# Loads of the residual rows in a three-stage kernel: issued by GpSimd instead of SyncE

## The chip, the cores and the metric

The kernel runs on one core of a Trainium2 chip. The metric is the device time of one execution in microseconds; for the kernel before it is the median of three runs. A core has TensorE (PE, matmuls), VectorE (DVE), ScalarE (ACT), GpSimd (POOL) and SyncE (SP), each with an instruction stream of its own that runs in order. They wait for each other by semaphores. SyncE does no arithmetic here; it issues DMAs. ACT issues DMAs as well, between its activations. All transfers of the core run on the same 16 DMA engines.

## The reference

The inputs are x and a context of 32 sequences x 512 rows x 512 columns, and a feed-forward layer with 2048 hidden columns.

```
r_t  = 0.9 * r_(t-1) + ctx_t * ctx_t              # scan over the 512 rows of a sequence
x2   = x + layernorm(x) * r
a    = quantize_uint8(layernorm(x2))              # one scale: the maximum over everything
h    = relu(a @ quantize_int8(w1).T + bq1)
hq   = quantize_uint8(h)                          # one scale: the maximum over everything
out  = x2 + hq @ quantize_int8(w2).T + bq2
```

The two scales cut the work into three stages: x2 must be complete before its quantized form can be made, and h must be complete before its own.

## The kernel before

Stage one (to about 349 us) makes x2 of every sequence and stores it in `x2_scratch` in HBM; GpSimd does small row statistics here and nothing afterwards. Stage two (to about 830 us) loads x2 again, quantizes it, forms the first product and keeps its unscaled sums in pieces that the text calls pairs: 128 partitions x 1024 fp32, 512 KB, 8 of them for a sequence. Those of 30 sequences go to `hidden_scratch` in HBM (240 pairs), those of the last two, the held ones, stay in SBUF.

Stage three, in which the change lies, walks over the sequences in turns, the two held ones first. In a turn s:

- ACT scales and rounds 8 pairs, half a pair per activation (L589), into a ring `hq` of 12 halves. Pairs come from a ring `hload` of 30 places. After the second half of a pair ACT issues the load of the pair 13 places on in the order of HBM (L570), and this one is needed 29 pairs later, since 16 held pairs lie ahead of all of them. The first 14 are loaded by SyncE before the stage, the other 226 by ACT in this way.
- PE forms the second product: 64 matmuls of 128x512 (L877), into four of the eight PSUM banks; turns take the two halves of PSUM by turns, so turn s may write a bank when DVE has read it for turn s - 2.
- DVE adds the bias to the x2 of the turn (`add_bias`, L761), then takes the sums from PSUM (`scale_out`, L752) and adds them (`add_out`, L766), four row tiles each. In DVE's stream stand, for turn s, first all outputs of turn s - 1, then `add_bias` of turn s.
- x2 of a turn lies in one of three slots of `work`. The result is formed in the same slot and stored from there. So the slot of turn s + 3 is free for its load only when the store of turn s has landed.

Loads (L349) and stores (L353), 1.05 MB each, are both issued by SyncE, in one stream: the store of turn s, then, after a wait for that store to land, the load of turn s + 3, then the store of turn s + 1. The last turn is stored in four parts (L370). The load of turn 2 (x2 of turns 0 and 1 is there from stage two) is issued ahead of the loop.

Of the kernel before, what the change touches and what calls it, by code (L numbers as in the profile page):

```python
# [39 lines left out]
HELD = 2  # L40
# [8 lines left out]
def wait_count(eng, sem, count):  # L49

    if isinstance(count, int) and count <= 0:
        return
    eng.wait_ge(sem, count)


def build(nc, x, ctx_in, w1, b1, w2, b2, out):
    NB, S, D = x.shape
    F = w1.shape[0]
    NI = S // P
# [8 lines left out]
    turns_c = held + stored  # L68
# [5 lines left out]
    def copy_index(b, q):  # L74
        return copied.index(b) * NP2 + q
# [11 lines left out]
    x2_dram = nc.dram_tensor("x2_scratch", [NB, P, ROW], F32, kind="Internal").ap()  # L87

    with ExitStack() as es:
# [3 lines left out]
        def sem(name):  # L93
            return es.enter_context(nc.semaphore(name))
# [63 lines left out]
        x2c = x2t  # L158
# [58 lines left out]
        x_scaled = sem("x_scaled")  # L217
# [13 lines left out]
        x2c_loaded = [sem(f"x2c_loaded{n}") for n in range(3)]  # L231
        bias_added = sem("bias_added")
        out_ready = sem("out_ready")
        out_stored = [sem(f"out_stored{n}") for n in range(3)]
# [6 lines left out]
        def batches(eng, step, peeled=0):  # L241

            for j in range(STRAIGHT):
                step(j, j % XS, j // XS)
            with eng.Fori(AHEAD, NG - peeled) as g:
                for n in range(XS):
                    step(g * XS + n, n, g)
            for j in range(NB - peeled * XS, NB):
                step(j, j % XS, j // XS)

        def is_first(j, n=1):
            return isinstance(j, int) and j < n

        def load_ctx(eng, j, n):
            eng.dma_start(ct[n], ctx_rows[bass.ds(j, 1)].rearrange("b p i d -> (b p) i d")).then_inc(ctx_loaded[n], 16)

        def weight_halves(j):

            at = {1: (0, 0), 2: (0, 1), 5: (1, 0), 6: (1, 1)}.get(j) if isinstance(j, int) else None
            return [at] if at else []  # L260
# [15 lines left out]
        def stores_in(n):  # L276

            return len(range(n, NLOAD, NKEEP))

        def out_slot(s):  # L280

            return (NB - HELD + s) % 3
# [5 lines left out]
        def stores_until(s):  # L288

            return len([m for m in range(s + 1) if out_slot(m) == out_slot(s)])  # L290
# [10 lines left out]
        @block.sync  # L301
        def _(sp):
            def store_x2(j, n):
                sp.wait_ge(x2_done, (j + 1) * NI)
                sp.dma_start(x2_dram[bass.ds(j, 1)].rearrange("b p m -> (b p) m"),
                             xt[n].rearrange("p i d -> p (i d)")).then_inc(x2_stored[n], 16)

            def load_x2(t):
                sp.dma_start(x2t[t % 3].rearrange("p i d -> p (i d)"), x2_dram[t]).then_inc(x2_loaded[t % 3], 16)

            def phase_a(j, n, g):
                if is_first(j):
                    load_ctx(sp, 0, 0)
                if isinstance(j, int) and j == XS - 1:
                    sp.wait_ge(dve_step, 1)
                if not is_first(j, XS):
                    sp.wait_ge(x2_stored[n], g * 16)
                sp.dma_start(xt[n], x_rows[bass.ds(j, 1)].rearrange("b p i d -> (b p) i d")).then_inc(x_loaded[n], 16)
                for w, h in weight_halves(j):
                    rows = (NF, KD)[w]  # L320
                    part = slice(h * rows // 2, (h + 1) * rows // 2)
                    sp.dma_start(w_stage[w].rearrange("p (c d) -> p c d", c=rows)[:, part, :],
                                 (w1_rows, w2_rows)[w][:, part, :]).then_inc(w_loaded[w][h], 16)
                if isinstance(j, int) and j == 2:
                    sp.dma_start(brow[:, :], b1_rows).then_inc(b_loaded, 16)
                    sp.dma_start(brow2[:, :], b2_rows).then_inc(b_loaded, 16)
                if not is_first(j, 2):
                    store_x2(j - 2, (n - 2) % XS)

            batches(sp, phase_a)  # L330
            store_x2(NB - 2, XS - 2)
            store_x2(NB - 1, XS - 1)
            sp.wait_ge(w_int, 8)
            for t in range(3):
                load_x2(t)

            for n, b in enumerate(stored):
                for q in range(NP2):
                    c = copy_index(b, q)
                    sp.wait_ge(h_copied, c + 1)  # L340
                    sp.dma_start(h_dram[n, q], hkeep[c % NKEEP].rearrange("p n t -> p (n t)")).then_inc(h_stored[c % NKEEP], 16)


            def load_x2c(s):
                if stores_until(s) > 1:
                    sp.wait_ge(out_stored[out_slot(s)], 16 * (stores_until(s) - 1))
                else:
                    sp.wait_ge(x_scaled, (NB - 2) * NI)
                sp.dma_start(x2c[out_slot(s)].rearrange("p i d -> p (i d)"), x2_dram[turns_c[s]]).then_inc(x2c_loaded[out_slot(s)], 16)  # L349

            def store_out(s):
                sp.wait_ge(out_ready, (s + 1) * NI)
                sp.dma_start(out_rows[turns_c[s]], x2c[out_slot(s)]).then_inc(out_stored[out_slot(s)], 16)  # L353

            for n in range(NKEEP):
                sp.wait_ge(h_stored[n], 16 * stores_in(n))
            sp.wait_ge(kept_maxed, NLOAD)
            for c in range(NKEEP):
                sp.dma_start(hload[c].rearrange("p n t -> p (n t)"), h_dram[c // NP2, c % NP2]).then_inc(h_loaded[c], 16)
            for s in range(HELD, 3):  # L360
                load_x2c(s)
            for s in range(len(turns_c) - 1):
                store_out(s)
                if s + 3 < len(turns_c):
                    load_x2c(s + 3)

            last = len(turns_c) - 1
            for i in range(NI):
                sp.wait_ge(out_ready, last * NI + i + 1)
                sp.dma_start(out_rows[turns_c[last], :, i, :], x2c[out_slot(last)][:, i, :]).then_inc(tail_stored, 16)  # L370
            sp.wait_ge(tail_stored, 16 * NI)
            for n in range(3):
                sp.wait_ge(out_stored[n], 16 * len([m for m in range(last) if out_slot(m) == n]))
# [3 lines left out]
        def _(gp):  # L377
# [18 lines left out]
            def row_stats(pw, st, mean, done, base):  # L396

                n = st.shape[1]
                me, mo, ve, vo = (st[:, :, k] for k in (1, 4, 2, 5))
                t = [pw[:, k, :] for k in range(8)]  # L400
                gp.tensor_tensor(t[0], me, mo, ALU.add)
                gp.tensor_tensor(t[1], ve, vo, ALU.add)
                gp.tensor_tensor(t[2], me, mo, ALU.subtract).then_inc(done, 1)
                gp.wait_ge(done, base + 1)
                gp.tensor_tensor(mean, t[0], half[:, 0:n], ALU.mult)
                gp.tensor_tensor(t[3], t[1], per_row[:, 0:n], ALU.mult)
                gp.tensor_tensor(t[4], t[2], half[:, 0:n], ALU.mult).then_inc(done, 1)  # L407
                gp.wait_ge(done, base + 2)
                gp.tensor_tensor(t[5], t[3], eps[:, 0:n], ALU.add)  # L409
                gp.tensor_tensor(t[6], t[4], t[4], ALU.mult).then_inc(done, 1)  # L410
                gp.wait_ge(done, base + 3)
                gp.tensor_tensor(t[7], t[5], t[6], ALU.add).then_inc(done, 1)  # L412
                return t[7]

            def second_stats(j, n):

                cols = bass.ds(j * NI, NI)
                wait_count(gp, stats2_ready, j)
                gp.wait_ge(stats2_in, j + 1)
                mean = pw2[:, 8, :]  # L420
                var = row_stats(pw2, st2[:, n], mean, ln2_step, j * 4)
                gp.wait_ge(ln2_step, j * 4 + 4)
                gp.tensor_tensor(pw2[:, 9, :], var, var, ALU.add)
                gp.tensor_tensor(zrow[:, cols], rowmax[:, n, :], mean, ALU.subtract).then_inc(stats2_used, 1)  # L424
                gp.tensor_tensor(mean2[:, cols], pw2[:, 0, :], half[:, :], ALU.mult)
                gp.tensor_tensor(rstd2[:, cols], var, neg_half[:, :], ALU.pow).then_inc(stats2_ready, 1)  # L426
# [23 lines left out]
            batches(gp, phase_a)  # L450
            second_stats(NB - 2, XS - 2)
            second_stats(NB - 1, XS - 1)


        @block.scalar
# [466 lines left out]
```

## Time and profile before

| | us |
|---|---|
| median of 3 runs (lowest, highest) | 1315.63 (1314.29, 1317.24) |
| the profiled execution | 1313.3 |
| its span, first to last instruction | 1311.5 |

| engine | busy us | share of the span | instructions |
|---|---|---|---|
| PE | 1229.3 | 94% | 5386 |
| ACT | 993.6 | 76% | 1403 |
| DVE | 908.9 | 69% | 1314 |
| POOL | 291.2 | 22% | 777 |

The DMA engines moved 460.23 MB, 351 GB/s over the span. Busy time counts instructions on an engine's datapath; waits and DMA issues are not in it, and have rows of their own ("SPq", "ACTq") in the timeline. Matmuls are pipelined, so a row of the timeline that merges many gives their time in sum better than a mean of single ones. A view by windows gives for each stretch the busy time of each engine with the number of instructions in it, then the granted clock, the DMA share and GB/s. In a wait, "A <- B" means that A stood idle until B released it; B is inferred, and a time in which an engine's own queue was held by a DMA issue can be put down to another engine.

### The profile page before, as it was taken

The page shows a single profiled execution, that of the slowest core. Times are in us where ns is not written, and L with a number is a line of the kernel's source. Part 1 is how long each engine was busy: PE and PEld are TensorE (multiplying, and loading weights), DVE is VectorE, ACT ScalarE, POOL GpSimd, SP SyncE. Part 2 cuts the span into 40 slices and gives each one's busy share as a digit, 9 for nine tenths or more (in the row PEclk, how much of TensorE's full clock was granted, in tenths as well). Part 3 has the DMA queues.
Part 4 walks back from the last instruction along what each step waited for, and adds up shares of the span by engine and source line. Part 5 has one row for each costly group of instructions (what it writes and reads, how often), then busy time and mean ns, then how long its engine had stood idle before and what let it go on. Part 6 is the DMA issues. An engine that isn't in the chain of part 4 may idle for free.

```text
span 1311.5 us, 17101 instructions
## 1 busy us (share of the span) xinstructions
PE 1229.3 (94%) x5386; PEld 562.2 (43%) x5386; DVE 908.9 (69%) x1314; ACT 993.6 (76%) x1403; POOL 291.2 (22%) x777
## 2 busy tenths in 40 slices
PE   6768999999599999999999999799999999989998
PEld 3333434343344444444444444344444444333333
DVE  5979999999577777777777777465454444444466
ACT  6687878787677777777777776778888787787774
POOL 2969999999500000000000000000000000000000
PEclk9888999999799999999999999899999999999999
DMA  9987999997489999999999998699999999999986
GB/s 355 343 325 261 344 332 346 339 334 287 193 308 362 352 350 362 364 357 345 362 362 362 350 355 322 227 354 417 415 415 416 415 415 416 416 415 415 416 297 219
DMA packets 136128, 460.23 MB, mean 351 GB/s; under 512 B 10853, under 2 KB 10873, under 8 KB 123513
## 3 DMA queue, kind: packets, MB, share of 16 engines
q1 hardware_dynamic: 82968, 277.91, 54.1%
q10 hardware_dynamic: 53088, 181.42, 39.1%
q8 instruction: 39, 0.64, 0.2%
q14 instruction: 33, 0.26, 0.0%
HBM read 266.35 MB, written 192.94 MB: 350 GB/s over the span
## 4 chain that ended last, share of the span: by engine, by line
PE 50%; DMA 18%; POOL 18%; issue 6%; DVE 4%; ACT 3%; POOLq 1%; ACTq 0%; DVEq 0%; SPq 0%
PE ps L835 34%; PE ps L877 12%; DMA out_dram<-work 12%; DMA work<-x_scratch 6%; PE ps L857 2%; POOL rstd L426 2%; POOL pw L410 2%; POOL pw L412 2%; POOL pw L409 2%; DVE work L766 2%; PE ps L814 1%; POOL rstd L444 1%; DVE work L761 1%; POOL pw L407 1%; POOL zrow L424 1%
## 5 line engine op out<-in xcount | busy, mean ns | idle before, releaser
L877 PE MATMUL ps<-w2T,xq 128*128 128x512 f16 x2048 | 451.9, 381 | 17.6 <-DVE work L752 9.9
L835 PE MATMUL ps<-xq,w1T 128*128 128x512 f16 x2048 | 449.4, 380 | 1.4 <-DVE xq L713 1.4
L589 ACT ACTIVATE xq<-xq,hb,hs 128x512 f16<-128x512 f32 x494 | 359.3, 802 | 92.9 <-PE ps L877 81.3
L704 DVE TENSOR_REDUCE work<-xq 128x2 f32<-128x1024 f32 x255 | 311.0, 1220 | 126.6 <-ACT xq L542 126.6
L542 ACT ACTIVATE xq<-ps 128x1024 f32<-128x1024 f32 x255 | 261.2, 1024 | 123.0 <-PE ps L835 122.8
L814 PE MATMUL ps<-xq,work 128*128 128x512 f32 x640 | 290.0, 610 | 30.1 <-ACT xq L477 19.7
L877 PEld LDWEIGHTS ps<-w2T,xq 128*128 128x128 f16 x2048 | 197.9, 98 | 271.6 <-ACT xq L589 21.9
L835 PEld LDWEIGHTS ps<-xq,w1T 128*128 128x128 f16 x2048 | 199.5, 98 | 237.4 <-issue 2.9
L814 PEld LDWEIGHTS ps<-xq,work 128*128 128x128 f32 x640 | 122.4, 195 | 195.3 <-issue 144.5
L761 DVE TENSOR_TENSOR work<-work,bq_bc 128x512 f32<-128x512 f32 x128 | 79.8, 685 | 165.4 <-DMA work<-x_scratch 165.4
L477 ACT ACTIVATE xq<-ps,rstd 128x512 f32<-128x512 f32 x128 | 78.0, 689 | 60.4 <-POOL rstd L444 56.0
L752 DVE TENSOR_TENSOR work<-ps,cs_bc 128x512 f32<-128x512 f32 x128 | 86.1, 687 | 48.9 <-PE ps L877 41.7
L622 DVE SCALAR_TENSOR_TENSOR xq<-xq,mean 128x512 f32<-128x512 f32 x128 | 96.1, 791 | 21.6 <-ACT xq L477 21.5
L548 ACT ACTIVATE work<-work,qb,zrow 128x512 f16<-128x512 f32 x128 | 102.6, 806 | 5.1 <-DVE qb L695 2.8
L630 DVE CUSTOM_DVE_ANT_0 xq<-xq 128x512 f32<-128x512 f32 x128 | 88.2, 689 | 0.0
L766 DVE TENSOR_TENSOR work<-work 128x512 f32<-128x512 f32 x128 | 84.7, 681 | 0.4
L627 DVE BATCH_NORM_STATS2 st<-xq 128x6 f32<-128x512 f32 x128 | 84.6, 681 | 0.0
L507 ACT ACTIVATE xq<-xq 128x2048 f32<-128x2048 f32 x32 | 60.8, 1899 | 6.1 <-DMA xq<-in_ctx_dram 5.8
L655 DVE BATCH_NORM_STATS2 st<-xq 128x6 f32<-128x512 f32 x64 | 40.4, 672 | 9.6 <-DMA xq<-in_x_dram 9.6
L468 ACT ACTIVATE work<-xq,st 128x512 f32<-128x512 f32 x64 | 45.3, 707 | 0.0
L465 ACT ACTIVATE work<-xq 128x512 f32<-128x512 f32 x64 | 40.8, 637 | 4.6 <-DMA xq<-in_x_dram 3.6
L713 DVE COPY xq<-ps 128x2048 f16<-128x2048 f16 x32 | 38.9, 1214 | 2.5 <-PE ps L857 2.5
(103 smaller groups left out, 536.7 us busy)
## 6 DMA issues: line engine op xcount, KB each, us to landing
hidden_scratch<-xq SPq DMA_DIRECT2D x240, 512.0 KB, 6.0
xq<-hidden_scratch ACTq DMA_DIRECT2D x218, 512.0 KB, 19.5
work<-x_scratch SPq DMA_DIRECT2D x33, 1024.0 KB, 8.3
xq<-in_x_dram SPq DMA_DIRECT2D x32, 1024.0 KB, 7.7
x_scratch<-xq SPq DMA_DIRECT2D x32, 1024.0 KB, 5.8
xq<-in_ctx_dram ACTq DMA_DIRECT2D x31, 1024.0 KB, 5.5
out_dram<-work SPq DMA_DIRECT2D x31, 1024.0 KB, 15.1
work<-x_scratch ACTq DMA_DIRECT2D x29, 1024.0 KB, 7.7
```

Source lines behind the costliest of these rows:

```text
L542: act.activation(into, pair_banks(b, q), ACT.Copy).then_inc(h_copied, 1)
L548: act.activation(qi[:, i, :], x2t[t % 3][:, i, :], ACT.Relu, bias=qb[:, t * NI + i:t * NI + i + 1], scale=qa[:, t * NI + i:t * NI + i + 1] ...
L589: act.activation(hq[c % HQ], src[:, c % 2, :], ACT.Relu, bias=hb[:, q:q + 1], scale=hs[:, q:q + 1]).then_inc(h_scaled, 1)
L622: dve.scalar_tensor_tensor(rs[n % 2][:, i, :], xt[n][:, i, :], mean1[:, n, i:i + 1], rs[n % 2][:, i, :], ALU.subtract, ALU.mult).then_inc( ...
L630: dve.tensor_tensor_reduce(xt[n][:, i, :], rs[n % 2][:, i, :], xt[n][:, i, :], 1.0, -3.0e38, ALU.add, ALU.max, rowmax[:, n, i:i + 1]).then ...
L704: dve.tensor_reduce(hmax[:, b * NF + 2 * q:b * NF + 2 * q + 2], src, AX.X, ALU.max).then_inc(kept_maxed, 1)
L752: dve.tensor_tensor(ot[:, i % 2, :], acc_bank(s, i), cs2_bc[:, :], ALU.mult).then_inc(acc_read, 1)
L761: dve.tensor_tensor(x2c[out_slot(s)][:, i, :], x2c[out_slot(s)][:, i, :], bq2_bc[:, :], ALU.add).then_inc(bias_added, 1)
L766: dve.tensor_tensor(x2c[out_slot(s)][:, i, :], x2c[out_slot(s)][:, i, :], ot[:, i % 2, :], ALU.add).then_inc(out_ready, 1)
L814: last = pe.matmul(ps[:, i, :], decay_mat[:, (i - k) * P:(i - k + 1) * P], ct[n][:, k, :], start=(k == 0), stop=(k == i))
L835: last = pe.matmul(bank, w1T[:, k, f * P:(f + 1) * P], xq_rows(b, k), start=(k == 0), stop=(k == KD - 1))
L877: last = pe.matmul(acc_bank(s, i), src[:, i * P:(i + 1) * P], w2T[:, q, :], start=first, stop=final)
```

## The change

The function `load_x2c` and the loop that calls it for turns 2 to 31 move from SyncE's stream to the end of GpSimd's. The waits in it are the same: for turn 2 that ACT has scaled 30 sequences in stage two, for the others that the earlier store out of that slot has landed. SyncE keeps the stores, and the waits of DVE are as they were.

```diff
-            def load_x2c(s):
-                if stores_until(s) > 1:
-                    sp.wait_ge(out_stored[out_slot(s)], 16 * (stores_until(s) - 1))
-                else:
-                    sp.wait_ge(x_scaled, (NB - 2) * NI)
-                sp.dma_start(x2c[out_slot(s)].rearrange("p i d -> p (i d)"), x2_dram[turns_c[s]]).then_inc(x2c_loaded[out_slot(s)], 16)
-
...
-            for s in range(HELD, 3):
-                load_x2c(s)
             for s in range(len(turns_c) - 1):
                 store_out(s)
-                if s + 3 < len(turns_c):
-                    load_x2c(s + 3)
...
             second_stats(NB - 2, XS - 2)
             second_stats(NB - 1, XS - 1)
+
+            def load_x2c(s):
+                if stores_until(s) > 1:
+                    gp.wait_ge(out_stored[out_slot(s)], 16 * (stores_until(s) - 1))
+                else:
+                    gp.wait_ge(x_scaled, (NB - 2) * NI)
+                gp.dma_start(x2c[out_slot(s)].rearrange("p i d -> p (i d)"), x2_dram[turns_c[s]]).then_inc(x2c_loaded[out_slot(s)], 16)
+
+            for s in range(HELD, len(turns_c)):
+                load_x2c(s)
```

## Rows read from the trace of the kernel before

**Rows 1.** Windows, stage three; last columns: clock, DMA share, GB/s
```profile
868.00:1262.00 394.00, 379.76 (x1734) 166.91 (x1733) 193.83 (x311) 314.41 (x432) 0.00 (x0) 1.00 1.03 414
920.00:960.00 40.00, 40.00 (x187) 18.15 (x186) 20.38 (x32) 33.06 (x47) 0.00 (x0) 1.00 1.03 415
1262.00:1311.50 49.50, 42.84 (x197) 18.73 (x194) 35.98 (x58) 28.86 (x40) 0.00 (x0) 0.99 0.67 215
```

**Rows 2.** PE: chain of waits (first row), timeline: start, us, work
```profile
852.64 112.25 PE ps L877 x520
...
1102.50 0.39 PE L877 MATMUL ps<-w2T,xq 128*128 128x512 f16 x1 [0.53 <-ACT xq L589]
1106.49 2.94 PE L877 MATMUL ps<-w2T,xq 128*128 128x512 f16 x12 [0.30 <-DVE work L752]
1263.57 2.94 PE L877 MATMUL ps<-w2T,xq 128*128 128x512 f16 x12 [0.68 <-DVE work L752]
1266.87 39.02 PE L877 MATMUL ps<-w2T,xq 128*128 128x512 f16 x180 [0.35 <-DVE work L752]
```

**Rows 3.** Waits in stage three: us in total, times, longest
```profile
DVE work L761 <- DMA work<-x_scratch: 165.4, 25, 8.9
ACT xq L589 <- PE ps L877: 83.6, 64, 3.2
```

**Rows 4.** Timeline of SyncE's queue, two turns
```profile
983.85 0.43 SPq L353 DMA_DIRECT2D out_dram<-work  x1
999.79 0.33 SPq L349 DMA_DIRECT2D work<-x_scratch  x1
1000.16 0.43 SPq L353 DMA_DIRECT2D out_dram<-work  x1
```

**Rows 5.** DMA issues of 870 to 1242; last: landing of L349 after 1262
```profile
work<-x_scratch SPq DMA_DIRECT2D x24, 1024.0 KB, 8.3
out_dram<-work SPq DMA_DIRECT2D x24, 1024.0 KB, 15.4
...
DMA to landing us min/median/max: 6.1/6.3/6.5
```

**Rows 6.** Timeline of ACT and its queue
```profile
1082.44 4.07 ACTq L570 DMA_DIRECT2D xq<-hidden_scratch  x1
1086.61 0.81 ACT L589 ACTIVATE xq<-xq,hb,hs 128x512 f16<-128x512 f32 x1 [2.80 <-PE ps L877]
1086.66 1.58 ACTq L570 DMA_DIRECT2D xq<-hidden_scratch  x1
...
1093.04 0.33 ACTq L570 DMA_DIRECT2D xq<-hidden_scratch  x1
```

**Rows 7.** Queues (q10 ACT, q1 SyncE): packets, MB, share; to 1242, to 1312
```profile
q10 hardware_dynamic: 31308, 114.03, 70.5%
q1 hardware_dynamic: 16067, 49.97, 30.9%
...
q10 hardware_dynamic: 32544, 118.50, 62.5%
```

**Rows 8.** Windows of L589 (ACT, first two) and L877 (PE) alone
```profile
838.00:1100.00 262.00, 215.46 (x300) 0.99 1.01 402
838.00:1242.00 404.00, 326.81 (x451) 0.99 1.02 407
...
838.00:1100.00 262.00, 260.18 (x1193) 116.96 (x1193) 0.99 1.01 402
838.00:1242.00 404.00, 389.67 (x1769) 171.06 (x1769) 0.99 1.02 407
```

**Rows 9.** Timeline of DVE: the end of turn 0's output, and the last
```profile
860.40 1.28 DVE L766 TENSOR_TENSOR work<-work 128x512 f32<-128x512 f32 x2
...
1308.33 0.69 DVE L766 TENSOR_TENSOR work<-work 128x512 f32<-128x512 f32 x1
```

**Rows 10.** The page's 40 slices of the span: GpSimd
```profile
POOL 2969999999500000000000000000000000000000
```

## The prediction, made before the changed kernel was run

> **Words.** A turn is one sequence's second product: 64 matmuls and 16 ACT activations. It takes 8 pairs (512 KB each) of kept sums, which ACT loads, one x2 load and one output store of 1.05 MB each. Turns 0 and 1 need no loads of pairs; 226 pairs come through ACT's queue.
>
> **What bounds the kernel now.** I read the stage table first. From 868 to 1262 us the DMA engines are full: 415 GB/s in a 40 us slice, DMA share 1.03; PE is busy 96% of it. After 1262 they carry 215 GB/s [rows 1]. So the third stage has two bounds close together. PE runs free at 112.25 us for 520 matmuls, 0.2159 us each: 13.81 us a turn. It does so until 1102.50, where ACT first releases it; turn 19 starts at 1106.49 and turn 29 at 1263.57, 15.7 us each [rows 2]. The DMA bound is 8 x 0.524 + 2 x 1.049 = 6.29 MB a turn, 15.15 us at 415.
>
> Next, the waits: DVE stood 165.4 us for x2 loads [rows 3]. The SyncE timeline shows why. After the store at 983.85 SyncE does nothing until 999.79, issues the load, and 0.37 us later the next store, without a wait of its own [rows 4]: it was ready. The load of turn s+3 waits for the landing of store s (its slot), and store s+1 is queued behind that wait. A store lands in 15.4 us, a load in 8.3 [rows 5], both in one queue: one turn in about 15.7 us, whatever PE does.
>
> Third, and this decides the case: ACT's own queue. At 1082.44 issuing one pair load takes 4.07 us, at 1086.66 1.58; one that isn't held takes 0.33 (1093.04). The activation behind the first starts only at 1086.61 [rows 6], when the issue is over; the 2.80 us the view puts down to PE is this. So ACT is held when its queue is full. How full: by 1242 all 226 pairs are issued and 114.03 of 118.50 MB have landed [rows 7], so 4.47 MB are outstanding, 8.5 pairs. Yet pair loads are issued 29 pairs ahead of use: the data needed is there, and ACT stands in an issue. ACT's lead over PE: at 1100 it has started 302 activations (300 in the window, 2 ahead of it), 151.0 pairs, and PE 1194 matmuls (1193 and 1), 149.25 pairs: a lead of 1.75, and there PE's first stalls stand. At 1242 it is 226.5 against 221.25, a lead of 5.25 [rows 8]. ACT, then, was the limit around 1100, and from there DVE's x2 waits were.
>
> **The change, part by part.** (1) Removed from SyncE: 30 loads and their waits. Issue time is 0.33 us each, hidden in idle time, worth nothing. What counts is that store s+1 no longer waits for store s to land. It goes out when ready: 4.9 us after its turn's last matmul (turn 0's end is 856.8, that is 843 + 13.81 where 843 is 964.89 less 565 x 0.2159; DVE was done at 861.68 [rows 9]).
>
> (2) Added to GpSimd: 30 waits and 30 issues. GpSimd does nothing after its eleventh slice [rows 10]; nothing is queued behind its waits but further loads, whose slots are freed later. The first load, for turn 2, now goes out when the 30th sequence is scaled, before stage two ends; its data is used after 870. Worth nothing. Without an idle GpSimd each wait of some 10 us would stand ahead of its arithmetic.
>
> (3) What a load costs in GpSimd's queue no row shows. The nearest rows from both sides: 6.3 us landed in a quiet stretch, 15.4 for a store behind a load in a full one [rows 5]. A store alone in its queue should land in 6.5 to 9. Store s plus load s+3 take 9 + 8.3 + 1, or 9 + 15.4 + 1 = 25.4 us; the load is needed when turn s+2 is done, two turns or 27.6 us after store s was ready. So DVE's x2 waits go, with 2 to 9 us to spare. I take 8.3, its own row.
>
> (4) What is late next. With DVE out of the way SyncE and GpSimd move 2.10 MB in each turn of PE instead of one turn's worth in 15.7 us. At PE's free pace that leaves 415 x 13.81 - 2097 = 3634 KB for pairs, 6.9 where 8 are asked for. ACT's queue fills by 1.1 pairs a turn and its issues hold ACT. Before, x2 and output had 49.97 MB by 1242 [rows 7], about 1.8 MB in 13.81 us, and it filled by 0.5 a turn. So ACT falls behind sooner, at about turn 10 to 12 instead of 19, and then the pace is the DMA bound, 15.15 us.
>
> **The sum.** Let X be the time of the last pair issue, after which nothing holds ACT; before, 1241.8. By X the same pairs must have moved as before. Of x2 and output more has moved: with PE then at pair 224.75, turn 28.1 (ACT at 226.5, less the lead of 1.75 that a held ACT has), stores 0 to 26 and loads 3 to 28 have landed, 53 x 1.0486 = 55.6 MB, against 49.97. These 5.6 MB at 0.415 MB/us are 13.5 us: X = 1255.3. Left for PE are 256 - 224.75 = 31.25 pairs of 1.726 us, 53.9 us: PE ends at 1309.2. Before: 34.75 pairs, 60.0 us, from 1241.8 gives 1301.8, and 4.1 us of waits for DVE to the real end, about 1305.9 (39.02 us from 1266.87 [rows 2]). The drain behind PE (DVE's last work starts at 1308.33 [rows 9]) stays. So +3.3 us: the span goes from 1311.5 to 1314.8, the profiled execution from 1313.3 to 1316.6. The median shown is 2.3 above that execution; I forecast 1318.9 for it, +0.25%. What was gained at DVE is handed back because x2 traffic that was late, and finished in the half empty tail, now competes with the pairs.
>
> Errors of the sum: a lead off by half a pair, 0.9 us; one pair more outstanding at X (a load fewer in SyncE's and ACT's queues may leave room), 1.3 us less; a data rate off by 1%, 385 us of full traffic, 3.9 us. This case: 1313 to 1323.
>
> **Rivals.** A, faster: ACT isn't held any more, because the limit on its issues is shared with SyncE and the loads leave it. Then the lag of 1.1 pairs over 26 turns is 28 pairs, within the 29 issued ahead, and PE could run free to 843 + 32 x 13.81 = 1284.9. The bytes allow hardly less: left at 1242 are 4.5 MB of pairs [rows 7] and, of 32 stores and 29 loads (64.0 MB), 14.0 MB; less the last 1.6 that is 16.9 MB, 41 us, so 1283, and some 10 us for the last pair and the drain. A span of 1293, a median near 1297. Against it speaks that an issue of 1.58 us [rows 6] is about what a pair takes in the engines (0.524 MB at 415 less SyncE's share), so each issue waits for one pair to leave its own queue. For it, that SyncE's transfers may take the same places; no row tells. 12%.
>
> B, no change: a load in GpSimd's queue lands so late (over 27 us) that DVE waits on, and the pace stays 15.7. The row of 15.4 speaks against it. 1315.6, 8%. The Trainium skill has a rule with the same result: all engines' DMAs run on the same 16 DMA engines, and issuing from several saves only issue time (DMA: Bandwidth & Descriptors, Issuing engines are not separate DMA queues). By that rule the change is worth 0.33 us a turn beside idle time, nothing. The trace agrees about the shared engines (415 GB/s is full), but shows an order of waits in SyncE's stream that the rule doesn't speak of.
>
> C, slower by more: the third queue lowers the rate of all. Its place is the full stretch; 1% costs 3.9 us, and it decides from the first per cent on. The slice shown holds 415 [rows 1]; 2% gives 1327, 4% 1334. 18%. The Trainium skill says that DMA engines 7 and 15 are usually slower and guesses at descriptor rings that GpSimd writes into SBUF (DMA: Bandwidth & Descriptors, Latency and other measured facts); a pair load is done when its slowest engine is. No row here has such a queue.
>
> **How the numbers follow.** My case has 62%. 0.2%, 2.6 us, is about what a measurement of this kernel can tell from no change. In my case +3.3 with an error of about 3 gives 0.34 slower, 0.22 same, 0.06 faster. With A 0.12 faster, B 0.08 same, C 0.18 slower: 0.18, 0.30, 0.52. The range, 1309 to 1332, leaves out A and the far end of C.
>
> **What would show it.** Right: stores follow DVE's last work by under 1 us; GpSimd's loads start as a store lands; DVE's waits for x2 loads fall from 165 us to under 20; ACT's issues are longer in sum, the first over 1 us before 960; PE's stalls begin near 1000, released by ACT and not DVE; last pair issue near 1255; 415 GB/s held until about 1270, then a shorter tail. Wrong: issues of 0.33 us throughout (A), 160 us of DVE waits (B), 40 us slices at 405 GB/s or less (C).

## The result, and the profile after

| | before | after |
|---|---|---|
| median, us | 1315.56 (9 runs, 1312.85 to 1317.24) | 1318.06 (9 runs, 1317.53 to 1319.27) |
| ratio, 95% interval | | 1.0029 [1.0018, 1.0039] |
| span of the profiled execution, us | 1311.5 | 1315.7 |

The change makes the kernel slower by 0.29%. That is small, but the whole interval lies above 1. The transfers move as the change says. From the page of the changed kernel (span; GpSimd in 40 slices; the new queue with packets, MB and share):

```profile
span 1315.7 us, 17101 instructions
POOL 2859999999500000000000000000000000000000
...
q0 software_dynamic: 4320, 31.46, 5.8%
```

The 30 loads have left SyncE's queue for GpSimd's (q0, 31.46 MB), and GpSimd's busy share rounds to nothing after its eleventh slice, as in [rows 10] (the windows below count its issues as POOL: 27 in the full stretch, 14.52 us). The windows of stage three, in answer to [rows 1]:

```profile
868.00:1262.00 394.00, 376.37 (x1711) 165.71 (x1709) 204.36 (x324) 304.88 (x423) 14.52 (x27) 1.00 1.03 416
...
1262.00:1315.70 53.70, 48.14 (x224) 21.61 (x221) 27.96 (x44) 36.03 (x51) 1.08 (x2) 0.98 0.51 191
```

The full stretch carries 416 GB/s with a third queue in it, as much as with two. After 1262 the engines are emptier than before, 191 GB/s instead of 215: less was left over for the tail. PE is busy 376.37 us of the 394, against 379.76.

The waits of stage three, in answer to [rows 3] (us in total, times, longest):

```profile
POOL work L448 <- DMA out_dram<-work: 486.4, 29, 97.6
DVE work L751 <- PE ps L876: 209.3, 63, 8.2
ACT xq L588 <- PE ps L876: 84.4, 43, 4.2
PE ps L876 <- ACT xq L588: 19.4, 31, 2.0
```

DVE's 165.4 us of waits for x2 are gone from the list; what DVE waits for now is PE. PE waits for ACT, 31 times. The full list has no row in which ACT waits for a DMA from `hidden_scratch`: the pairs it needs are there.

DVE's last work of a turn, SyncE's store of it, GpSimd's next two loads with what released them, and then the landing times of the stores (L346) and of the loads (L448):

```profile
969.05 1.28 DVE L765 TENSOR_TENSOR work<-work 128x512 f32<-128x512 f32 x2
...
970.36 0.37 SPq L346 DMA_DIRECT2D out_dram<-work  x1
...
972.12 0.54 POOL L448 DMA_DIRECT2D work<-x_scratch  x1 [13.96 <-DMA out_dram<-work]
984.49 0.54 POOL L448 DMA_DIRECT2D work<-x_scratch  x1 [11.83 <-DMA out_dram<-work]
...
DMA to landing us min/median/max: 4.3/13.9/15.4
...
DMA to landing us min/median/max: 5.0/9.3/10.7
```

DVE ends at 970.33 and the store is issued at 970.36. The load at 984.49 follows 0.3 us after this store has landed, 14.1 us after its issue; the load at 972.12 was released by the store of the turn before. This answers [rows 4, 5]: no store waits for another one.

ACT and its queue, in answer to [rows 6]; the last row is the last pair issue of the kernel:

```profile
948.40 1.62 ACTq L569 DMA_DIRECT2D xq<-hidden_scratch  x1
...
1244.75 5.48 ACTq L569 DMA_DIRECT2D xq<-hidden_scratch  x1
...
1250.33 0.81 ACT L588 ACTIVATE xq<-xq,hb,hs 128x512 f16<-128x512 f32 x1 [4.20 <-PE ps L876]
...
1255.32 0.33 ACTq L569 DMA_DIRECT2D work<-hidden_scratch  x1
```

The first issue of over 1 us comes at 948.40; before the change it was at 1004.63. The one at 1244.75 takes 5.48 us and the activation behind it starts when it is over, at 1250.33. In sum the 226 issues take 149.5 us beyond 0.33 us each; before, 115.8. From 985 us to 1245 one issue in each turn takes 4.2 to 5.9 us and a few behind it 1 to 2 us; the stops of PE below come once a turn too.

PE in stage three, in answer to [rows 2]:

```profile
853.22 152.65 PE L876 MATMUL ps<-w2T,xq 128*128 128x512 f16 x706
1007.07 0.39 PE L876 MATMUL ps<-w2T,xq 128*128 128x512 f16 x1 [1.19 <-ACT xq L588]
1007.77 13.77 PE L876 MATMUL ps<-w2T,xq 128*128 128x512 f16 x63 [0.32 <-ACT xq L588]
...
1129.48 0.39 PE L876 MATMUL ps<-w2T,xq 128*128 128x512 f16 x1 [1.08 <-ACT xq L588]
...
1144.81 0.39 PE L876 MATMUL ps<-w2T,xq 128*128 128x512 f16 x1 [0.86 <-ACT xq L588]
...
1251.20 0.39 PE L876 MATMUL ps<-w2T,xq 128*128 128x512 f16 x1 [1.44 <-ACT xq L588]
1251.91 58.23 PE L876 MATMUL ps<-w2T,xq 128*128 128x512 f16 x269 [0.31 <-ACT xq L588]
```

PE runs free to three quarters of turn 11 (152.65 us) and is then released by ACT, in most turns once, with a further small stop of 0.3 us. From 1129.48 to 1144.81 is one turn, 15.3 us; the 16 turns from 1007.07 to 1251.20 take 15.26 each. Before, PE ran free 95 us longer and then lost 1.9 us a turn. In that stage the waits of the kernel before put 9.9 us of PE's idle time down to DVE (19 times) and 5.1 to ACT (7 times); that this pace was set by DVE's wait for x2 is shown by serial_free below.

The queues at 1255 us (q10 ACT, q1 SyncE, q0 GpSimd), then the windows of ACT's activations and of PE's matmuls up to there, in answer to [rows 7, 8]:

```profile
q10 hardware_dynamic: 31227, 113.74, 68.0%
q1 hardware_dynamic: 14236, 28.30, 17.5%
q0 software_dynamic: 3744, 27.26, 15.7%
...
838.00:1255.00 417.00, 326.15 (x452) 0.99 1.01 407
...
838.00:1255.00 417.00, 396.52 (x1794) 174.26 (x1795) 0.99 1.01 407
```

### The profile page after: what moved, and what is told of

It reads as the page before. It is cut to its first block and busy times, and to the rows that moved or that the text cites. A ratio compares the mean times of both kernels' runs of the same rounds, so it can differ in the third digit from the quotient of the medians.

```text
span 1315.7 us, 17101 instructions
## 1 busy us (share of the span) xinstructions
PE 1230.5 (94%) x5386; PEld 563.6 (43%) x5386; DVE 910.7 (69%) x1314; ACT 990.8 (75%) x1403; POOL 307.2 (23%) x807
## 3 DMA queue, kind: packets, MB, share of 16 engines
q0 software_dynamic: 4320, 31.46, 5.8%
## 5 line engine op out<-in xcount | busy, mean ns | idle before, releaser
L448 POOL DMA_DIRECT2D work<-x_scratch x30 | 16.4, 545 | 912.5 <-DMA out_dram<-work 486.4
## 6 DMA issues: line engine op xcount, KB each, us to landing
xq<-hidden_scratch ACTq DMA_DIRECT2D x218, 512.0 KB, 20.1
out_dram<-work SPq DMA_DIRECT2D x31, 1024.0 KB, 13.9
```

## The experiments

Two theories. **H**, for "held": PE is limited by ACT, and ACT is held in the issues of its own full queue, for pairs that it needs only 29 pairs later. The change frees DVE, but makes x2 traffic prompt, which fills ACT's queue sooner; so one hold takes the place of the other. **D**, for "data": PE goes at the pace at which bytes arrive, and the held issues are a symptom. Both give the changed kernel's 15.2 us a turn. They part where ACT no longer issues the pairs.

With the first three kernels the two holds can be set out in a table, each taken away alone and both together (medians, us; each ratio is to the kernel before as it ran beside that kernel, where its median was 1315.56 for the changed kernel and 1314.96 for the other three; so a difference between medians of the two groups is uncertain by some 0.6 us):

| | ACT issues the pairs | another engine issues them |
|---|---|---|
| SyncE's serial order | before: 1315.6 | serial_free: 1312.1, 0.9982 [0.9972, 0.9992] |
| stores and x2 loads prompt | after: 1318.1, 1.0029 [1.0018, 1.0039] | act_freed: 1295.6, 0.9856 [0.9832, 0.9880]; pairs_gp: 1297.5, 0.9877 [0.9852, 0.9902] |

### act_freed: ACT issues the stores, SyncE the pairs

```diff
 SyncE, instead of the stores:
+            for c in range(NKEEP, NLOAD):
+                sp.wait_ge(h_scaled, 2 * (c - NKEEP + 1))
+                sp.dma_start(hload[c % NRING]..., h_dram[c // NP2, c % NP2]).then_inc(h_loaded[c % NRING], 16)
 ACT, in its loop over half pairs c:
-                if c % 2 == 1 and NKEEP <= pair + NKEEP - 1 < NLOAD:
-                    load_kept(pair + NKEEP - 1)
+                if c % NF == 3 and c >= 2 * NF:
+                    store_out(c // NF - 2)
```

> The changed kernel, with the two hardware queues swapped between their issuers: SyncE issues the 226 pair loads, ACT issues the 31 output stores (that of turn s after the fourth activation of turn s + 2, when it is ready) and the four last parts; GpSimd keeps the x2 loads. The bytes are the same. Theory H (the changed kernel's ACT is held in its pair issues by its full queue, while the pairs it needs lie ready; x2 traffic is prompt): ACT is free, SyncE is held instead and holds nobody, PE runs at 13.8 us a turn to near the end, and the bytes are the bound: 1293 to 1301 us. Theory D (PE simply goes at the pace at which bytes arrive, 15.2 us a turn, and the held issues are a symptom without effect): no change from the changed kernel, 1316 to 1320.

Measured: 1295.64 us, 22.4 less than the changed kernel. Its PE, then its waits in stage three, then the window of the full stretch:

```profile
853.80 415.00 PE L875 MATMUL ps<-w2T,xq 128*128 128x512 f16 x1922
1269.64 0.39 PE L875 MATMUL ps<-w2T,xq 128*128 128x512 f16 x1 [0.84 <-ACT xq L582]
...
ACT xq L582 <- DMA xq<-hidden_scratch: 13.2, 18, 2.5
PE ps L875 <- ACT xq L582: 4.3, 5, 2.0
...
868.00:1282.00 414.00, 412.84 (x1912) 186.92 (x1911) 228.09 (x360) 338.63 (x470) 15.67 (x29) 1.00 1.03 416
```

PE runs 415 us without a stop, until near the end of stage three. The DMA engines carry the same 416 GB/s as in the changed kernel. So, as long as the reserve lasts, PE isn't tied to the pace at which bytes arrive: it takes 13.8 us a turn where a turn's bytes take 15.2, and lives on the 29 pairs of reserve that ACT's hold kept it from using in the changed kernel. D falls. SyncE is held now (147 of its 226 issues take over 1 us), and holds nobody. Only near the end, from 1207 us on, does ACT wait for pairs that haven't landed, 13.2 us in all; there the bytes begin to bind. This version beats both kernels.

### serial_free: the kernel before, GpSimd issues the pairs

```diff
 GpSimd, at its end:
+            for c in range(NKEEP, NLOAD):
+                gp.wait_ge(h_scaled, 2 * (c - NKEEP + 1))
+                gp.dma_start(hload[c % NRING]..., h_dram[c // NP2, c % NP2]).then_inc(g_loaded[c % NRING], 16)
 ACT:
-                if c % 2 == 1 and NKEEP <= pair + NKEEP - 1 < NLOAD:
-                    load_kept(pair + NKEEP - 1)
```

> The kernel before, with the 226 pair loads issued by GpSimd instead of ACT; SyncE keeps stores and x2 loads in its old order. Theory H: ACT is free, but the order in SyncE (each store waits for the one before to land) still paces DVE at about 15.7 us a turn, so taking away ACT's hold alone is worth little: 1308 to 1317, with some 150 us of DVE waits for x2 and PE released by DVE. Theory D: 1314 to 1318, the same as before. A rival S, that SyncE's order never limited and ACT's hold alone did: 1293 to 1301.

Measured: 1312.05 us. PE, and the waits:

```profile
854.64 268.66 PE L879 MATMUL ps<-w2T,xq 128*128 128x512 f16 x1244
1123.55 11.40 PE L879 MATMUL ps<-w2T,xq 128*128 128x512 f16 x52 [0.25 <-DVE work L754]
1136.81 2.94 PE L879 MATMUL ps<-w2T,xq 128*128 128x512 f16 x12 [1.86 <-DVE work L754]
...
1262.34 2.94 PE L879 MATMUL ps<-w2T,xq 128*128 128x512 f16 x12 [1.21 <-DVE work L754]
...
DVE work L763 <- DMA work<-x_scratch: 155.7, 24, 8.9
PE ps L879 <- DVE work L754: 11.0, 17, 1.9
```

The first stop moves from 1102.50 to 1123.55, and it is DVE that ends it; DVE's waits for x2 are 155.7 us, against 165.4. From 1136.81 to 1262.34 are eight turns of 15.7 us, the pace of the kernel before, though no pair issue stands in ACT's stream. So ACT's hold was worth 2.4 us in the kernel before (1.1 to 3.7 by the interval of the ratio), and SyncE's order takes over 21 us later. This is H. S falls; D's no change is missed by only 2 us, and it is act_freed that decides against D.

### pairs_gp: GpSimd issues the pairs, ACT the x2 loads, SyncE the stores

```diff
 ACT:
+                if c % NF == 4 and c >= 3 * NF:
+                    load_x2c(c // NF)
```

with the loads of the pairs on GpSimd as above.

> Three issuers another way round: GpSimd the 226 pair loads, SyncE the stores alone, ACT the x2 loads (that of turn s after the fifth activation of turn s, when the slot's store should have landed). Neither SyncE's order nor a full ACT queue is left. Theory H: as with ACT freed in the other way, 1293 to 1301. Theory D: 1314 to 1320. If a queue filled by GpSimd costs rate, this kernel, with 118 MB in it instead of 30, is slower than the other by several us, and a full stretch shows under 410 GB/s.

Measured: 1297.47 us. PE, and the window of the full stretch:

```profile
852.65 387.37 PE L883 MATMUL ps<-w2T,xq 128*128 128x512 f16 x1794
1240.34 0.39 PE L883 MATMUL ps<-w2T,xq 128*128 128x512 f16 x1 [0.32 <-ACT xq L595]
...
868.00:1282.00 414.00, 411.63 (x1901) 185.37 (x1900) 225.19 (x356) 338.15 (x468) 111.23 (x207) 1.00 1.03 415
```

Nearly the same gain in another arrangement (1.8 us less of it), so it isn't a property of SyncE's or ACT's queue. With four times as many bytes in GpSimd's queue as in the changed kernel the engines carry 415 GB/s. None of GpSimd's issues takes over 1 us, though its pairs land in 32.8 us in the median (20.1 in the changed kernel).

### quarter: the changed kernel with a quarter of each x2 load

```diff
-                gp.dma_start(x2c[out_slot(s)].rearrange("p i d -> p (i d)"), x2_dram[turns_c[s]])...
+                gp.dma_start(x2c[out_slot(s)][:, 0, :], x2_dram[turns_c[s]][:, 0:D])...
```

> The changed kernel with only one of four row tiles of each x2 load in stage three (262 KB instead of 1.05 MB; the other three tiles of the slot keep what lay there, so the output lacks part of x2). A turn moves 5.5 MB, 13.3 us at 415 GB/s, under PE's 13.8. Both theories H and D: ACT isn't held for long, PE runs free, its end is near 839.7 + 1.8 + 442 = 1284, the median 1291 to 1295. It measures what the x2 traffic costs in the changed kernel: some 24 us. A rival N, that something in GpSimd's queue other than its bytes holds PE: over 1305.

Measured: 1294.26 us. PE, the window, and the durations of ACT's issues (ns, min, median, max):

```profile
855.60 431.83 PE L876 MATMUL ps<-w2T,xq 128*128 128x512 f16 x2000
...
868.00:1262.00 394.00, 394.00 (x1827) 178.58 (x1826) 216.38 (x343) 327.38 (x456) 15.90 (x29) 1.00 0.97 378
...
L569 ACTq DMA_DIRECT2D xq<-hidden_scratch x218: 326/326/828, 840.6 to 1225.6; - x109
```

The output lacks three quarters of x2 here. With 23 MB less in the queues, PE's row runs over 2000 matmuls, no issue of ACT takes over 0.83 us, and the DMA share is 0.97. These bytes of x2 cost the changed kernel 23.8 us (1318.06 less 1294.26), though DVE waits for none of them. As act_freed carries all of them in 1295.6 us, they cost it through ACT's queue.

### early_wait: act_freed with a wait that ACT doesn't need

```diff
+                if c % 2 == 1 and NKEEP <= pair + 4 < NLOAD:
+                    act.wait_ge(h_loaded[(pair + 4) % NRING], 16 * ((pair + 4) // NRING + 1))
```

> The kernel in which SyncE issues the pair loads and ACT the stores (1295.6 us), plus one wait in ACT: after the second half of pair p it waits until the pair has landed that is used 20 pairs later, the one 9 issues behind the load that ACT itself would issue there. It makes ACT wait as a full queue of 8.5 pairs would, for data that it doesn't need yet; transfers and issuers stay. Theory H (it is this hold of ACT that costs the 22 us, not where the loads are issued): PE's stalls come back near turn 11 or 12, released by ACT, a turn takes 15.2 us, and the time is 1314 to 1321. Theory Q (the kernel was faster because pairs in SyncE's queue and stores in ACT's are served better): it stays under 1300.

Measured: 1316.18 us, ratio 1.0014 [1.0003, 1.0025]. PE, and the waits:

```profile
853.39 166.58 PE L877 MATMUL ps<-w2T,xq 128*128 128x512 f16 x771
1020.28 13.91 PE L877 MATMUL ps<-w2T,xq 128*128 128x512 f16 x63 [0.31 <-ACT xq L582]
...
1126.87 0.39 PE L877 MATMUL ps<-w2T,xq 128*128 128x512 f16 x1 [0.63 <-ACT xq L582]
...
1141.97 0.39 PE L877 MATMUL ps<-w2T,xq 128*128 128x512 f16 x1 [0.63 <-ACT xq L582]
...
DVE work L761 <- DMA work<-x_scratch: 116.0, 23, 7.0
ACT xq L582 <- DMA xq<-hidden_scratch: 59.1, 73, 2.2
PE ps L877 <- ACT xq L582: 16.6, 40, 2.0
```

The same transfers by the same issuers as in act_freed; one wait in ACT, for data used 20 pairs later, costs 20.5 us. PE's stops are back, released by ACT; 1126.87 to 1141.97 is 15.1 us. Q falls. The imitation isn't exact: ACT also issues the stores here, and where ACT is late they are late; DVE waits 116.0 us for x2, which it doesn't in the changed kernel. The list has no row in which PE waits for DVE, though.

### split_pairs: the changed kernel, each pair load as two halves

```diff
+                for h in range(2):
+                    act.dma_start(hload[c % NRING][:, h, :], h_dram[c // NP2, c % NP2][:, h * S:(h + 1) * S])...
```

> The changed kernel with each of ACT's pair loads issued as two of half a pair (256 KB, 2 KB a partition). It asks what fills the queue. If it is bytes: ACT is held again at 8.5 pairs, and the time is 1317 to 1320. If it is transfers or their pieces, twice as many for the same bytes: it is held at about 4.3 pairs, first before 925 us, the last issue comes some 5 us later for the bytes that are no longer outstanding, and the time is 1321 to 1327.

Measured: 1339.40 us, ratio 1.0186 [1.0164, 1.0208]: slower than both expectations. PE, the window of 1000 to 1200 us, and the landing of half pairs and stores:

```profile
855.03 69.71 PE L877 MATMUL ps<-w2T,xq 128*128 128x512 f16 x322
925.41 0.39 PE L877 MATMUL ps<-w2T,xq 128*128 128x512 f16 x1 [0.68 <-ACT xq L589]
...
1000.00:1200.00 200.00, 183.31 (x809) 76.76 (x808) 94.98 (x151) 150.68 (x204) 7.02 (x13) 1.00 1.05 401
...
xq<-hidden_scratch ACTq DMA_DIRECT2D x436, 256.0 KB, 11.2
out_dram<-work SPq DMA_DIRECT2D x31, 1024.0 KB, 9.6
```

Two things act. ACT is held with 8.2 half pairs outstanding in the median (4.3 to 10.2), 4.1 pairs; its first issue of over 1 us is at 853.15, and PE's first stop at 925.41. So it isn't bytes that fill the queue, but transfers, or pieces of them, of which half a pair has as many rows as a pair; the two aren't told apart. And the rate is 401 GB/s instead of 416, which I hadn't reckoned with: over 385 us of full traffic 3.7% is 14 us, and with the 5 us expected for the lower fill the sum is 1337. That these two terms make up the whole is worked out, not shown by a run.

## Why the prediction was right

The forecast was 1318.9 us, +3.3 by the sum; the medians differ by 2.5 and the spans by 4.2. Both the path (DVE freed, ACT held sooner, less left for the tail) and the size came out. Point by point:

- **The order of waits in SyncE** is gone, and with it DVE's 165 us. Forecast under 20 us, found none. The stores go out within 0.1 us of DVE's end.
- **What is late next: ACT's queue.** Forecast: first issue over 1 us before 960, PE's stalls from about turn 10 to 12, near 1000, released by ACT. Found: 948.40, turn 11, 1007.07, ACT. The pace of the DMA bound, 15.15 us a turn, was 15.26.
- **The balance of bytes at X.** Forecast: stores and x2 loads have moved 55.6 MB when the last pair is issued, X = 1255.3, and ACT's lead is 1.75 pairs. Found: 28.30 + 27.26 = 55.56 MB and 1255.32. The lead was 1.75 at 1255.00 (226 pairs, 452 halves, less 224.25, 1794 matmuls), but at the issue itself the counts are 453 and 1795, a lead of 2.1. So close an agreement in X is in part luck: the stage began 0.74 us later than in the trace of before (PE's long row starts at 853.22 instead of 852.48), and the rate was 416 instead of 415, which nearly cancels it.
- **PE's end.** Forecast 1309.2, found 1251.91 + 58.23 = 1310.1; 0.65 of the 0.9 us is that lead: at X PE was at pair 224.4 instead of 224.75. The late start is already in X. It is no more than scatter: in the eight kernels PE's long row starts between 852.48 and 855.60.
- **A term that was wrong: how fast a store lands.** I gave a store alone in its queue 6.5 to 9 us. It took 13.9 in the median, hardly less than the 15.4 it took behind a load. The load took 9.3, near the 8.3 chosen. Together with the issue of 0.54 that is 23.7 us of the 27.6 there were while PE ran free, so it cost nothing. With a load of 15.4, the upper bound of that part, it would have been 29.8: DVE would have waited until ACT was held, and from then on two turns give 30.5. The margin given as 2 to 9 us was about 4 with the measured landings, and below zero at that bound.
- **The rivals.** A (ACT isn't held any more) fell by the trace and is what act_freed then made, by other means: 1295.6, where A's sum said 1297. B fell: x2 loads land in 9.3 us. C fell: 416 GB/s, and 415 in pairs_gp with 118 MB in GpSimd's queue. The runs turned on an issuer's order of waits and on an issuer that is held: with the same transfers on the same engines, who issues them was worth 22 us. The Trainium skill's rule that issuing from several engines saves only issue time (DMA: Bandwidth & Descriptors, Issuing engines are not separate DMA queues) agrees with the rates here, 415 to 416 GB/s whoever issues. By it the change is worth nothing and act_freed as well; measured were +0.29% and -1.4%, so the time doesn't follow it, unless the time for which an issue is held, up to 5.86 us, is counted as issue time. Of the engines 7 and 15 that the Trainium skill calls usually slower (same page, Latency and other measured facts) no run shows a cost in the total rate.

What stays open: whether the queue is full by transfers or by their pieces, and how queues share the engines. The store's landing went from 13.9 to 9.6 us when ACT's pairs came in rows of 2 KB instead of 4 KB, as if a queue's share went with the size of its pieces; no run is on that alone.

## What to carry to other kernels

A DMA issue can hold the engine that makes it. Where transfers are issued far ahead of use and DMA is full, as here, let an engine that computes nothing issue them and be held. Two waits that end close together hide each other: removing ACT's hold alone gave -0.2%, SyncE's order alone +0.3%, both together -1.4%. Before freeing a late stream, ask whose transfers it will crowd: its lateness may be what leaves them room.

## What the runs showed of the hardware

- A hardware queue let its issuer go on until about 8 to 9 pair loads of 512 KB (128 rows of 4 KB) were outstanding: in the median of the held issues 8.5 before, with SyncE's loads and stores beside them, 8.3 after with stores alone, 8.8 for SyncE in act_freed; single held issues of these kernels lie between 7.3 and 10.1. So the limit goes with the issuer's own queue. With 256 KB loads it was 8.2 of these (4.3 to 10.2).
- GpSimd's queue took 226 pair loads without an issue of over 1 us in both kernels that gave them to it; in pairs_gp up to 27.7 pairs (issues made, less bytes landed) were outstanding, three times what held ACT and SyncE.
- Loads in rows of 2 KB instead of 4 KB lowered the rate of the full stretch from 416 to 401 GB/s.
- An activation that follows a held issue shows its idle time as a wait for PE (4.20 us at 1250.33), although the issue of 5.48 us from 1244.75 is what it waited for. The duration of the issue is what to read.
